# Second attention of a two-layer transformer kernel: two normalisations move from VectorE to GpSimd, and GpSimd's order around them changes

## The reference, cut to what matters

```
h = _layernorm(x) * (1 + ca) + sa
x = x + ga * _L1_attn_ref(h, ...)      # features of q and k, sums, v, output product, layer norm of h + attn_out
h = _layernorm(x) * (1 + cb) + sb
x = x + gb * _L1_ffn_ref(h, ...)       # top 2 of 16 experts, and a shared one
...
q = jax.nn.elu(q) + 1.0 ; k = jax.nn.elu(k) + 1.0
q = q / jnp.sum(q, -1, keepdims=True) ; k = k / jnp.sum(k, -1, keepdims=True)
```

## Time and profile before

| | |
|---|---|
| median of 3 runs | 548.93 us (548.8 to 549.23) |
| the profiled execution | 548.54 us, of which its span on the core is 546.8 us |
| busy share of the span | PE 81%, DVE 67%, ACT 48%, POOL 46% |
| second attention | from about 212 us of the span to about 414 us |
| DVE busy from 215 to 415 us | 171.34 us of 200 |
| POOL busy from 215 to 415 us | 109.62 us of 200 |

### The profile page before, as it was taken

How to read it: one execution, slowest core, us unless ns; L and a number is a source line. 1 busy time by engine, 2 the same in 40 slices (tenths; PEclk the granted TensorE clock), 3 DMA queues, 4 the chain that set the end, 5 groups by cost and what they waited for, 6 DMA issues and landing times.

```text
span 546.8 us, 10536 instructions
## 1 busy us (share of the span) xinstructions
PE 440.9 (81%) x2430; PEld 303.7 (56%) x2430; DVE 364.3 (67%) x1181; ACT 264.4 (48%) x666; POOL 250.2 (46%) x322
## 2 busy tenths in 40 slices
PE   4889733999999992799889889988657779999950
PEld 3667611777777770256555555545524456777730
DVE  6879940355555552679999999999644445656636
ACT  3357610444444430757777678667232115656520
POOL 3105771143444444336348558457549002656560
PEclk9999755899999996989999999999778999999985
DMA  7999874212122604834122500000003020222107
GB/s 240 348 272 247 243 144 81 55 51 55 47 58 55 223 16 127 205 69 96 38 59 70 132 10 21 0 22 21 15 25 99 19 60 22 78 76 79 49 12 231
DMA packets 63420, 51.52 MB, mean 94 GB/s; under 512 B 9180, under 2 KB 54733, under 8 KB 63234
## 3 DMA queue, kind: packets, MB, share of 16 engines
q1 hardware_dynamic: 56434, 40.86, 29.2%
q0 software_dynamic: 5056, 8.48, 4.6%
q10 hardware_dynamic: 1872, 1.52, 1.2%
HBM read 37.19 MB, written 15.60 MB: 97 GB/s over the span
## 4 chain that ended last, share of the span: by engine, by line
PE 46%; DVE 31%; issue 11%; POOL 4%; DMA 4%; ACT 2%; SPq 0%; DVEq 0%; POOLq 0%; ACTq 0%
PE bank L1505 15%; PE bank L1520 8%; PE bank L1597 4%; PE bank L1513 4%; PE bank L1659 4%; DVE qk_sums L1202 4%; POOL sorted_tokens L716 3%; DVE work L1195 3%; DVE big L1195 3%; DVE work L1239 3%; PE bank L1498 2%; PE bank L1551 2%; DVE ln_stats L258 2%; PE bank L1651 2%; PE bank L1627 2%
## 5 line engine op out<-in xcount | busy, mean ns | idle before, releaser
L725 POOL DMA_INDIRECT results<-work x94 | 91.7, 975 | 139.3 <-DVE work L1172 76.3
L1158 DVE TENSOR_TENSOR work<-bank,bias_big 128x512 f32<-128x512 f32 (+1 forms) x94 | 57.1, 608 | 94.0 <-PE bank L1505 92.5
L857 ACT ACTIVATE work<-bank,mcol 128x128 f32<-128x128 f32 x94 | 43.0, 458 | 115.7 <-PE bank L1498 115.7
L1551 PE MATMUL bank<-late,work 128*128 128x512 f32 x192 | 94.6, 621 | 2.4 <-ACT work L873 2.2
L1505 PE MATMUL bank<-big,work 128*128 x188 | 91.4, 568 | 3.6 <-ACT work L857 3.6
L1551 PEld LDWEIGHTS bank<-late,work 128*128 128x128 f32 x192 | 33.9, 195 | 30.6 <-issue 27.0
L1520 PE MATMUL bank<-big,work 128*128 x376 | 49.7, 275 | 0.0
L1520 PEld LDWEIGHTS bank<-big,work 128*128 128x128 f32 x376 | 45.8, 192 | 0.1
L716 POOL DMA_INDIRECT sorted_tokens<-late,router_at x32 | 31.1, 973 | 27.1 <-DVE late L1107 17.6
L766 POOL DMA_INDIRECT sorted_tokens<-rows,router_at x32 | 31.2, 976 | 13.1 <-issue 7.9
L1505 PEld LDWEIGHTS bank<-big,work 128*128 128x128 f32 x188 | 28.8, 194 | 13.1 <-issue 13.1
(11 more groups left out here) (223 smaller groups left out, 984.5 us busy)
## 6 DMA issues: line engine op xcount, KB each, us to landing
work<-sorted_tokens SPq DMA_DIRECT2D x94, 65.0 KB, 1.8
big<-in_w SPq DMA_DIRECT2D x48, 88.0 KB
big<-in_W SPq DMA_DIRECT2D x1, 4096.0 KB
bias_big<-in_b SPq DMA_DIRECT2D x16, 256.0 KB
big<-results SPq DMA_DIRECT2D x16, 256.0 KB, 3.5
sorted_tokens<-zeros SPq DMA_DIRECT2D x2, 975.0 KB
sorted_tokens<-zeros SPq DMA_DIRECT2D x24, 65.0 KB
late<-in_WqkvbT SPq DMA_DIRECT2D x1, 1544.0 KB
```

Of the source, the lines that this page charges most:

```text
L725: pool.indirect_dma_start(ys[l], bass.IndirectOffsetOnAxis(xg[b][:, D:D + 1].bitcast(I32), 0), yo[b], None, bounds_check=TOPK * T - 1, oob ...
L857: act.activation(xgT[b % 2], bank[:, ends[b % 2], 0:P], ACT.Identity, bias=scale_shift[0], scale=scale_shift[1]).then_inc(e_xTc, 1)
L1158: dve.tensor_tensor(hb[b % 2][:, 0:width], bank[:, 1 + b % 2, 0:width], bias_big[:, bass.ds(e * width, width)], ALU.add).then_inc(e_hb, 1)
L1551: last = pe.matmul(bank[:, 2 * k + i, :], h3T[b], Wqkvb[:, k * HD + i * 512:k * HD + (i + 1) * 512], start=True, stop=True)
```

## The change

`scale3` and `norm5` leave DVE's list, and GpSimd runs them with the same instruction (`tensor_scalar`, subtract and multiply by numbers of the partition). On GpSimd they stand behind `product` and ahead of the sends, with lags that keep them at about the same point of the pipeline. `double1` moves with them: it stood first in the slot and now stands behind `norm5`, of the same tile.

```diff
+            def scale3(t, b, q):
+                after(pool, d_xT, t - 1)
+                ln_scale(pool, ln3, xt(t), t, b)
+
+            def norm5(t, b, q):
+                wait_rows_sent(pool, router1, t, b)
+                ln_scale(pool, ln5, xt(t), t, b)
+
...
             run_unrolled(NT, 4, [
-                (10, double1), (8, residual), (6, product), (11, send1(1)), (11, send1(0)), (1, add_results)])
+                (8, residual), (6, product), (9, norm5), (9, double1), (4, scale3), (11, send1(1)), (11, send1(0)),
+                (1, add_results)])
...
             run_unrolled(NT, 4, [
                 (3, feature(1)), (3, feature_sums), (7, picks[2]), (3, sums_product), (8, places[3]),
-                (6, norm5), (3, sigmoid_product), (3, sigmoid_inverse), (0, measure3), (3, sigmoid), (4, measure4),
-                (7, picks[3]), (3, qk_reduced), (4, moments4), (7, picks[4]), (3, coefficient), (1, scale3),
+                (3, sigmoid_product), (3, sigmoid_inverse), (0, measure3), (3, sigmoid), (4, measure4),
+                (7, picks[3]), (3, qk_reduced), (4, moments4), (7, picks[4]), (3, coefficient),
```

6 lines of the change are left out of this document (removed).

## The result

The changed kernel took 554.22 us (median of 4 runs, 553.5 to 556.16), the kernel before 548.96 us (4 runs, 548.8 to 549.23): a ratio of 1.0101, 95% interval 1.0075 to 1.0127. On another chip the same kernel had a ratio of 1.014 (1.0099 to 1.0181). The change made the kernel slower by some 5 us.

The account below looks back on a forecast made before the run. DVE was taken to bound the kernel from 245 us on. The terms, -4.9 + 1.9 + 4.6 + 0.7 + 0 = +2.3, taken as +2.2 on 548.54, gave 550.7, plus 0.4 for the median: 551.1 us, range 546.2 to 557.0.

Parts of the forecast that it names:

- late product: In three slots behind sends, POOL's product begins about 1.0 us late and holds DVE's L352: 1.9 us lost.
- What leaves DVE: From 245 us on, DVE saves 0.15 us for each of 12 scale3 and 0.24 for each of 13 norm5: 4.9 us.
- Collisions: Behind the product, POOL's moved scalings stop DVE's small two-input instructions: 0.35 us a slot, 13 slots, 4.6 us lost.
- POOL's new instruction: Each moved scaling on POOL takes 0.46 us, bounded by 0.297 (copy) and 0.91 (two passes of the two-input form).
- rival of the dear instruction: POOL's scaling takes 0.91 us, slots with sends 12.1, the product is 1.9 late: +9.8 us, 558.7 us; chance 0.13.
- The start: At the first scale3, behind three tiles' adds in POOL's list, PE starts 0.86 us later: 0.7 us lost.
- The end: norm5 of the last two tiles comes behind the last residual: put at 0, with 0.46 us either way.
- The signs to look for: Changed trace: L273 0.4 to 0.5 us, PE's start 216.0, product 1 us late, L352 over 0.6, 11.2 between products with sends.

Follow-up runs that it names:

- e8: The kernel before, DVE keeping both scalings, with two spare scalings of the same form added on POOL in each slot: 579.74 us, 1.0087 of the kernel before.
- e10: The changed kernel with the odd tile's sends one slot later, last in the slot, and norm5's wait cut to match: 548.25 us, 0.9976 of the kernel before.
- e3: The changed kernel with DVE's third pick (L352 in it) moved ahead of the sums of features: 559.65 us, 1.0226 of the kernel before.
- e2: The changed kernel with scale3 back on DVE, so POOL runs only norm5, with double1 behind it: median 553.41 us, 1.0076 of the kernel before.
- e1: The changed kernel with norm5 back on DVE and double1 where it was, so POOL runs only scale3: median 550.11 us, 1.0075 of the kernel before.
- e13: The same program as e10, run once more on another chip: 550.23 us, 1.0031 of the kernel before.
- e4: The changed kernel with the odd tile's sends moved to the head of the next slot: 555.86 us, 1.0147 of the kernel before.

## Why the prediction was right, and where its parts were wrong

I predicted 551.1 us (546.2 to 557.0), slower at 0.56. It was slower, and 554.2 lies in the range, 3 us above the forecast. The mechanism, a late product that holds DVE's L352 behind the slots with sends, and its place were the ones I named. Several sizes were wrong, in opposite directions, and that the sum came as near as it did is in part luck. One reading of the earlier trace rows was too kind as well: both of its stretches miss the sends, with POOL at 4.1 to 5.0 us of 10; from 310 to 320 us of the kernel before POOL is busy for 8.69.

**What leaves DVE: -4.9, measured -3.8 to -4.9.** In a slot with sends of the changed kernel (DVE's timeline below, which answers to the earlier trace rows) L1216 and L1221 start 0.28 us apart (0.43 before, I expected 0.20), and L1238 and L1248 0.21 (0.36 before, as expected). That is 0.15 + 0.15 = 0.30 a slot instead of 0.39, or 13 x 0.15 + 12 x 0.15 = 3.75 us. But part of the 0.28 may be a collision. Between e8, in which DVE keeps both, and the changed kernel, with nearly the same work on POOL, the slot with sends differs by 10.40 - 10.01 = 0.39 us, just what I had forecast.

```profile
311.58 0.17 DVE L1216 TENSOR_TENSOR sums<-qk_sums 128x16 f32<-128x16 f32 x1
311.67 0.17 DVE L435 TENSOR_TENSOR gates<-router_ex,router_se 128x4 f32<-128x4 f32 x1
311.86 0.26 DVE L1221 SCALAR_TENSOR_TENSOR sums<-eb,sums 128x16 f32<-128x16 f32 x1
...
314.02 0.18 DVE L1238 SCALAR_TENSOR_TENSOR sums<-sums 128x16 f32<-128x16 f32 x1
314.23 0.69 DVE L1248 TENSOR_TENSOR work<-bank,sums 128x512 f32<-128x512 f32 x1
```

**Collisions: +4.6, measured +1.3 to +2.7.** Of all the steps this is the one that failed. I had taken 0.35 us a slot from the rows on which POOL's two-input instructions stop DVE. The timeline above stands beside POOL's scaling (311.64 to 312.44) and has L435 and L1221 with 0.17 and 0.26 us, against the 0.15 and 0.16 of the earlier trace rows, 0.1 us together. The slot is 10.01 instead of 10.19: 0.30 saved and 0.1 given back, or, with e8 as the measure, 0.39 saved and 0.21 given back; times 13 that is 1.3 or 2.7 us instead of 4.6. The net is the same by either, 3.75 - 1.3 = 2.45 and 4.9 - 2.7 = 2.2, and fits the 2.0 to 2.7 us that e10 gains from the third sums to the sixteenth. The Trainium skill (SBUF — State Buffer, Who interferes with whom) says that a VectorE instruction with two SBUF inputs contends with a GpSimd instruction that reads SBUF, for ports that are an exclusive lock; the traces agree for POOL's product (1.94 us of L352, 1.56 of L1216 in e3) and not for its scaling, which reads SBUF too, and where L1221 began inside it and ended 0.32 us before it. Here the measurement decides.

**POOL's new instruction: 0.46, measured 0.80.** Between the bounds of 0.297 and 0.91 I took the row that seemed nearest, and the upper end was nearer. The Trainium skill (GPSIMD Engine Reference, Engine selection) puts one-input work at roughly line rate; the copy may bear that out, with 0.30 us against 0.46 for two inputs, but at this size the scaling does not, with 0.55 to 0.81.

**The late product: 1.0 us late in three slots for +1.9, measured up to 2.05 us in four slots for +4.7**, net of what these slots save, and a fifth at the end. The way from product to product was to be 10.18 + 0.99 = 11.17 and is 12.02: two instructions that are 0.34 dearer, and 0.17 more of small gaps between instructions. The fourth and the fifth pair of slots have no adds, a way that is 1 us shorter; with 0.46 they would have been 0.2 late at most, with 0.80 they are 1.10 and 0.68 late. The rival of the dear instruction had this part nearly right (12.1 us, and 1.9 late) and came out too slow as a whole by the collisions, 9.1 us in it.

**The start: +0.7, measured +1.8.** To the first sums 1.77 us were lost, by `scale3` (e2, in which DVE keeps it, has 13.51 us there); 0.34 of the difference is the dearer instruction. The second slot was 1.62 us shorter, by PE's clock as shown above. I had not foreseen that, and it hid most of this loss.

**The end: 0, measured +2.4.** I had counted an instruction and overlooked what stands ahead of it in POOL's queue. POOL at the last residual:

```profile
401.30 0.96 POOL L774 DMA_INDIRECT sorted_tokens<-rows,router_at  x1 [0.30 <-issue]
...
403.84 0.80 POOL L273 TENSOR_SCALAR rows<-xres,ln_mv,ln_r 128x128 f32<-128x128 f32 x1
```

PE, which waits for it:

```profile
404.89 0.45 PE L318 MATMUL bank<-ident,rows 128*128 128x128 f32 x1 [4.33 <-POOL rows L273]
```

DVE's scaling for the last residual was done at 401.15, and POOL was still sending until 402.26: 1.1 us. In e1 the sends end earlier and the last residual follows DVE's scaling at once (15.58 us behind the sixteenth sums, 16.76 in the changed kernel, 17.00 in e2, 14.43 in e10). Another 0.35 is the late product of the sixteenth slot. Of the remaining 0.95, 0.54 stand in PE's rows ahead of that last residual. The same eight matmuls took, before, in the changed kernel and in e1:

```profile
389.06 1.09 PE L1565 MATMUL bank<-ident,work 128*128 128x128 f32 x8 [0.89 <-DVE work L1239]
```

```profile
392.66 1.73 PE L1566 MATMUL bank<-ident,work 128*128 128x128 f32 x8 [0.89 <-DVE work L1248]
```

```profile
388.88 1.97 PE L1570 MATMUL bank<-ident,work 128*128 128x128 f32 x8 [0.89 <-DVE work L1248]
```

The granted clock around them was 0.77, 0.59 and 0.50. The rest, some 0.4 us, comes further down the chain, from POOL's longer L273 and from L1598 (3.76 us for four, 3.47 before). So e1, which has neither the late product nor the sends in its way, still takes 1.5 us more there than the kernel before. Over the 30 us behind the sixteenth sums the mean clock is the same in the three, 0.77; what differs is which instructions the low clock falls on. That differs from one execution to the next, as e10 and e13 show, and whether any of this share is the change's own is not shown.

**The signs to look for.** POOL's L273 rows were to be 0.4 to 0.5 (0.80); PE's first row at 216.0 (215.85, with a first add that came 0.57 us earlier); the product 1 us late (2.05); L352 over 0.6 (1.94); 11.2 us from product to product (12.0); L435 or L1221 longer than 0.16 (0.17 and 0.26); DVE's busy time the same (364.3 and 364.9). The kinds were right, the sizes were off.

By the marks of the two traces the sum is now 0.15 (start and second slot) + 4.72 (slots behind sends) - 1.05 (the other slots) + 2.40 (end) - 0.42 (ahead of the attention and behind the counts) = 5.8 us. The forecast of +2.2 came near because a collision term that was 2 to 3 too large and a gain by PE's clock that was in no term stood beside a late product, an end and a start that were 2.8, 2.4 and 1.1 too small.

## What to carry to other kernels

An engine that is busy for 55% of a stretch (109.62 of 200 us) may be full in every second slot: before work is moved to it, lay the way from one instruction that must be on time to the next end to end, and see what is left (here nothing: 10.18 of 10.19 us). When an engine holds a lock, ask when its long instruction ends, not how much it works in all: from the third sums to the sixteenth the same change lost 3.6 us with the sends in one slot and gained 2.0 with the sends in two. When work is moved within a list as a remedy, count the way between the same two marks again: in e4 the sends changed their slot and still lay between the same two products. And look at the granted clock of both traces before a difference is put down to the change.

## What the runs showed of the hardware that I had not expected

- A `tensor_scalar` on GpSimd, 128x128 in float32, takes 0.55 us with one constant, 0.62 with one scalar for each partition, 0.67 with two constants, 0.81 with two scalars for each partition; a copy takes 0.30 and a product of two tensors 0.46. At this size one input is dearer than two.
- GpSimd's `tensor_tensor` stops DVE's small instructions with two SBUF inputs until it ends (L352 0.17 to 1.94 us, L1216 0.16 to 1.56); its `tensor_scalar` of 0.8 us makes each of them longer by 0.16 at most (e8, and 0.12 in the changed kernel).
- Two executions of one program, equal within 0.04 us over 153 us, parted by 2.8 us in the next 30, with PE's granted clock at 0.50 for 20 us in one and at 0.84 in the other. Two such places in this kernel, the second slot of the attention (1.6 us) and its end, can win or lose 0.3% each.
